# Two tables instead of one for the tiles of an expert layer, and one register load of four offsets for every pair of tiles

## The reference

```
x = x + conv_block(layernorm_over_channels(x))   # depthwise 3x3, taps from pooled means and maxima
t = to_tokens(x)                                 # 32768 tokens of 128 numbers
n = layernorm(t)
w, e = top_2(n @ Wg + bg); w = softmax(w)        # two of 8 experts for each token
t = t + sum over the two e of  w_e * (gelu(n @ W1[e] + b1[e]) @ W2[e] + b2[e])   # 128 -> 512 -> 128
out = from_tokens(t)
```

## Time and profile before

| | |
|---|---|
| median of 3 runs | 1646.42 us (1645.32 to 1646.55) |
| the profiled execution's own time | 1645.53 us |
| its span, from first to last instruction | 1643.7 us |
| instructions in the trace | 45749 |
| mean granted TensorE clock | 0.949 |
| busy share of the span | PE 92%, DVE 82%, PEld 68%, ACT 65%, POOL 60% |

### The profile page before, as it was taken

The page is one execution under the profiler, slowest core; times in us unless marked ns, Lnnn a source line. Parts: engine busy times, 40 slices in busy tenths (PEclk is TensorE's granted clock), DMA queues, the critical chain, the costliest instruction groups (busy, mean ns, idle before and its releaser), DMA issues.

```text
span 1643.7 us, 45749 instructions
## 1 busy us (share of the span) xinstructions
PE 1506.0 (92%) x12254; PEld 1118.7 (68%) x12255; DVE 1347.3 (82%) x2727; ACT 1070.7 (65%) x2410; POOL 989.9 (60%) x1061
## 2 busy tenths in 40 slices
PE   5899999999999489999999999999999999999766
PEld 2454554545455329888888888888888888888654
DVE  3568888888888849889899898989989899998644
ACT  5577777777775317777777777777777777777400
POOL 1004554555555665777777777777777777777500
PEclk7999999999999559999999999999999999999976
DMA  4201212222121181111111111111111111110099
GB/s 132 77 29 63 78 63 70 64 70 75 55 78 39 42 158 49 43 40 43 45 44 40 39 40 41 44 43 39 45 46 39 45 41 45 44 43 8 27 401 391
DMA packets 61927, 115.80 MB, mean 70 GB/s; under 512 B 15278, under 2 KB 38986, under 8 KB 61879
## 3 DMA queue, kind: packets, MB, share of 16 engines
q1 hardware_dynamic: 37080, 62.29, 12.7%
q0 software_dynamic: 18176, 34.27, 6.7%
q10 hardware_dynamic: 6624, 18.69, 3.1%
HBM read 60.22 MB, written 58.61 MB: 72 GB/s over the span
## 4 chain that ended last, share of the span: by engine, by line
POOL 37%; issue 21%; DMA 5%; POOLq 2%; PE 1%; DVE 1%; SPq 0%; ACT 0%
POOL xn L472 14%; POOL token_out L484 13%; POOL yt L479 8%; DMA ye<-token_out 4%; POOL rows_by_pair L460 1%; PE psV L979 1%; POOLq L484 1%; DMA rows_by_pair<-rows,idx 0%; POOLq L478 0%; POOLq L480 0%; POOLq L482 0%; PE psT L784 0%; POOLq L470 0%; SPq L391 0%; DMA rt<-rows_by_pair 0%
## 5 line engine op out<-in xcount | busy, mean ns | idle before, releaser
L1294 DVE TENSOR_TENSOR gl<-g,gh 128x512 f16<-128x512 f32 x624 | 493.5, 829 | 90.2 <-ACT gh L684 84.5
L460 POOL DMA_INDIRECT rows_by_pair<-rows,idx x256 | 272.0, 1063 | 323.5 <-issue 200.1
L484 POOL DMA_INDIRECT token_out<-yt,rt x312 | 339.9, 1090 | 186.5 <-POOL yt L479 132.7
L799 PE MATMUL psV<-lp,diag 128*128 128x512 f32 x576 | 275.1, 610 | 18.5 <-ACT cv L568 17.6
L684 ACT ACTIVATE gh<-g 128x512 f16<-128x512 f32 x468 | 276.1, 624 | 17.3
L677 ACT ACTIVATE g<-psV 128x512 f32<-128x512 f32 x312 | 185.4, 598 | 132.2 <-PE psV L918 99.3
L677 ACT ACTIVATE g<-psT 128x512 f32<-128x512 f32 x312 | 183.1, 597 | 111.3 <-PE psT L918 77.6
L472 POOL TENSOR_SCALAR xn<-rt 128x128 f32<-128x128 f32 x312 | 239.6, 775 | 11.1 <-DMA rt<-rows_by_pair 7.5
L939 PE MATMUL psR<-wall,gh 128*128 x1248 | 223.9, 274 | 13.5 <-issue 8.1
L939 PE MATMUL psG<-wall,gh 128*128 x1248 | 223.0, 273 | 0.0
L940 PE MATMUL psG<-wall,gl 128*128 x1248 | 214.3, 219 | 0.0
(11 more groups left out here) (212 smaller groups left out, 2980.8 us busy)
## 6 DMA issues: line engine op xcount, KB each, us to landing
rt<-rows_by_pair SPq DMA_DIRECT2D x156, 133.0 KB, 2.1
xb<-in_x_dram SPq DMA_DIRECT2D x32, 512.0 KB, 3.5
ye<-token_out SPq DMA_DIRECT2D x32, 512.0 KB, 7.8
out_dram<-oe ACTq DMA_DIRECT2D x32, 512.0 KB, 8.4
token_out<-yt,rt POOLq DMA_INDIRECT x312, 2.3
rows_by_pair<-rows,idx POOLq DMA_INDIRECT x256, 2.4
stage<-in_L_ffn_W_dram SPq DMA_DIRECT2D x1, 2048.0 KB, 9.3
rows_by_pair<-pad_rows SPq DMA_DIRECT2D x15, 133.0 KB
```

The source lines that it names most:

```text
L460: gp.indirect_dma_start(rows_dram, bass.IndirectOffsetOnAxis(ap=idx[p][:, b:b + 1].bitcast(U32), axis=0), rows[p][:, b, :], None).then_inc ...
L484: gp.indirect_dma_start(y_dram, bass.IndirectOffsetOnAxis(ap=rt[r][:, b, ID:ID + 1].bitcast(U32), axis=0), yt[r][:, b, :], None, bounds_ch ...
L799: ins = te.matmul(psConv.rearrange("p (h w) -> p h w", w=WW), diag[k][:, m, :], lp[j][:, y:y + HH // 2, dx:dx + WW], start=(m == 0), stop= ...
L1294: v.tensor_tensor(gl[side][q][:, cols], g[side][:, cols], gh[side][q][:, cols], ALU.subtract).then_inc(lo_done, 1)
```

## The change

The table of eight numbers per tile becomes two tables of two numbers each: `row_t` (the first row, and a zero) and `off_t` (the two offsets). Both go out to DRAM and come back, as `tab` and `tab_off`. Two columns that nothing reads (the experts' numbers) go, and with them two conversions on VectorE. As a tile's two offsets now stand directly beside those of the next tile, TensorE loads four registers with one instruction, for two tiles, and does so in steps with an even number only.

More of the change, by code:

```diff
@@ L390, in _ @@
             for r in range(RING):
-                first = sp.value_load(tab[0:1, TW * r:TW * r + 1], min_val=0, max_val=NREG * CAP)
+                first = sp.value_load(tab[0:1, 2 * r:2 * r + 1], min_val=0, max_val=NREG * CAP)
                 load_rows(first, r)
@@ L394, in _ @@
                 for r in range(RING):
-                    first = sp.value_load(tab[0:1, bass.ds((RING * t + r) * TW, 1)], min_val=0, max_val=NREG * CAP)
+                    first = sp.value_load(tab[0:1, bass.ds((RING * t + r) * 2, 1)], min_val=0, max_val=NREG * CAP)
                     sp.wait_ge(y_out[r], 16 * TB * t)
```

## The result

The changed kernel takes 1603.11 us (median of four runs, 1602.37 to 1603.79) against 1646.49 us for the kernel before (four runs here, one more than above): a ratio of 0.9734 with an interval of 0.9720 to 0.9749, 43.4 us faster. The forecast was 1634 (1629 to 1648), and so it missed; the time is near that of the first rival (1601), to which I gave one chance in ten.

A forecast was written before the change was run, and what follows sets the result against it. TensorE's sequencer, too slow in the loop, was taken as the bound. Loop loads save 13.3 us, less 1 us for the lead, other terms nothing: 1646.42 - 12 = 1634.4, given as 1634, range 1629 to 1648.

The forecast's parts named there:

- the first rival: Loop's register load is a fixed trip: four registers cost about 538 ns, gaps vanish, time 1601; chance a tenth.
- What bounds the kernel: Tile stage: TensorE sets the pace; in the loop its sequencer's own work fills the 24.03 us round of four tiles.
- The load in the loop: Four registers take 1076 ns, like two loads together; 0.18 us saved per pair of tiles, 13.3 us over 37 rounds.
- my lower bound: Lowest price allowed for the loop's load of four: 538 ns, all of it the trip, the second pair free.
- The lead can be carried: In the loop, the sequencer's lead passes between tiles, reaching 1.0 to 1.2 us at the load; 1 us taken off.
- DVE and POOL follow: In the loop, DVE and POOL keep up with PE at about 5.93 us per tile; cost nothing.
- The written-out steps: Written-out steps and first load: together between 0 and 0.5 us saved; counted as nothing.
- The two tables: Before the tile stage: one more DMA out and one more in, covered by SP's wait; cost nothing.
- The cover of 14 us: On SP, time from issuing the table's way back (593.64) to the row DMAs (607.76), hiding the second table's transfer.
- A fixed trip: Rival for the loop's load: four registers cost about 538 ns, a round takes 22.8 us, time 1601; chance 0.10.
- POOL and DVE don't follow: Rival: in the loop they hold each other at 6.02 us per tile, time 1646 to 1648; chance 0.11.
- the lead is not carried: Rival: in the loop, the sequencer's lead stays at 0.68 us, 25 us lost, time 1671; chance 0.07.

The follow-up runs named there:

- two lumps: Changed kernel with its load of four registers split into two loads of two, both in the even step; 1645.25 us, ratio 0.9994.
- shifted by eight bytes: Changed kernel with TensorE's line of offsets beginning two words further on in SBUF, so loads miss the 16-byte place; 1631.91 us, ratio 0.9919.

## Why the prediction was wrong

**What bounds the kernel: right.** The gap behind the load is where a sequencer that is too slow on the whole is caught up with. The forecast's 0.116 us a step stood in no row. It is (24.03 - 4 x 0.60) / 186, the value that makes the sum come out, and so it proved nothing. The traces do (20 rounds of each): with each kind of step at its median from start to start (123 fused register operations at 0.124 us, 36 plain ones at 0.093, 16 on semaphores at 0.106, 10 moves at 0.087, the branch at 0.266, four loads at 0.596) a round before needs 23.8 of its 24.03 us, and no register operation takes over 0.18. The changed kernel's round needs 22.0 of 22.81 by the same count, and single steps stretch to 0.35: there the sequencer waits. The one-table kernel with four registers in each step, the kernel with two lumps and the one shifted by eight bytes came out at the sums of the sequencer's steps, within 0.1 us a round (23.22, 23.98 and 23.61 us).

**The load in the loop: this step failed.** "I take these as one line, 269 ns per register and nothing fixed. Four registers then take 1076 ns." It measured 332 ns. One register on one engine and two on another are two points; they can't show how a third length goes. Even my lower bound, 538 ns, was no bound: I took it as given that a load of four can't be faster than one of two. With 332 in the same sum a round needs 24.03 - 2 x 0.18 - 4 x 0.538 + 2 x 0.332 = 22.2 us of sequencer time. That is under the array's 22.8, so the array decides: 37 x 1.23 = 45.5, a time of 1601; the measured 1603.11 is 2 us above, and the later start of the stage (3.3 us) accounts for it.

The rule of the Trainium skill ("DMA: Bandwidth & Descriptors", Latency and other measured facts: a floor of about 600 ns for a `tensor_load`, unrolled by four to make up for it) pointed at the right time, and I gave it a tenth. Its figure doesn't hold here (298 ns for one word, 332 for four). That loading four at once can make up for the cost was in it; that this needs an aligned group was not. Its page "Runtime: NRT & Kernel Launch" (Instruction fetch mechanics) gives about 200 ns per register, even in bulk, for loads from HBM; the word-by-word loads here, from SBUF, are near that at 210 to 250 for each further word, the aligned four are not. No run here loads from HBM.

**The lead can be carried: right**, shown by the two lumps (23.98 us a round). The size of the gaps was near too: I had 0.3 and 0.6 us beyond the usual 0.11 for a load of 1.08 us; the shifted kernel has 0.17 (r = 2) and 0.61 (r = 0), for one of 1.00.

**DVE and POOL follow: right**, further than I asked of them, down to 5.70 us a tile. My reason for the short `xn` was wrong, though: it goes with `gl`, not with DVE's work as such.

**The written-out steps: nothing, as forecast. The two tables: probably not nothing, but some 3 us.** The cover of 14 us on SP was real for the tables' own transfers (596.45 against 611.09). What I didn't ask is whether their DMAs can make the last scatters land later. The traces lean that way, by the amounts above; by what means stays open.

**The rivals.** "A fixed trip" had the right time with the wrong price (538 ns for 332), and that is partly luck: with any load of four under about (22.80 - 21.52) / 2 = 0.64 us the array decides, and the time is the same. (21.52 us is the changed round without its loads, 24.03 - 2 x 0.18 - 4 x 0.538.) Nor is a load a fixed trip: one, two and three words take 298, 540 and 787 ns. I gave it a tenth because of a ratio of two that says nothing of a whole group of four. "POOL and DVE don't follow" and "the lead is not carried" are refuted.

## What to carry to other kernels

Load registers in whole groups of four words that begin on a 16-byte place, even where some of the words are of no use: here four cost less than two (332 against 538 ns), and eight bytes of misplacement made the load cost three times as much. Where a sequencer works out addresses for every matmul, add up its steps per round and set the sum against the array's time; the place of a gap tells where the sequencer was caught up with, not which of its steps is slow. And count the instructions of an experiment in its trace before reading its time: a load that nobody needs may not be there.

## What the runs showed of the hardware

- A register load on TensorE's sequencer took 298 to 313 ns for one word, 537 to 541 for two, 787 for three, 997 to 1001 for four that don't begin on a 16-byte place (counted from where the table's line began before it was moved), 331 to 337 for four that do, and 597 for eight that do.
- With these loads changed (and the register operations that belong to them), a round of four tiles went from 24.03 us to 22.81 (the array's own time), 23.22, 23.61 or 25.3.
- TensorE's sequencer could be over 1 us ahead of the array: 621.99 - 620.72 = 1.27 us in the written-out steps of the kernel before. In the kernel shifted by eight bytes the load behind an odd step started 1.15 us before the last matmul of `up` at r = 2, and its 998 ns cost a gap of 0.17 us; at r = 0 it was 0.71 us before, and the gap 0.61.
- In the loop of the kernel before, one register operation on TensorE's sequencer followed the other after 0.09 to 0.12 us; 190 instructions of its own in a round of four tiles made it slower than the array (24.03 against 22.81 us).
- An instruction of POOL on `xn` took 1.19 us beside DVE's `gl` and 0.44 us beside its `ya`.
